# Value ring of four, token-array zeroing on ScalarE's queue, and paired shared feed-forward

## What is computed

```python
# attention on xn = layernorm(x); 16 heads of 16; 16 global keys and a causal window of 32
scores = Q @ K.T * 0.25 + sparse_mask
x = x + softmax(scores) @ V @ Wo.T + xn
# feed-forward on h = layernorm(x)
x = x + h
topk_w, topk_idx = top_k(softmax(h @ gate_w.T), 6)      # 64 experts, weights renormalised
x = x + sum_over_chosen_experts(weight * (silu(h @ w_gate[e].T) * (h @ w_up[e].T)) @ w_down[e].T)
x = x + (silu(h @ sh_gate.T) * (h @ sh_up.T)) @ sh_down.T   # the shared feed-forward, width 352
```

## Time and profile before

| | |
|---|---|
| median of 3 runs | 650.39 us (646.25 to 652.29) |
| the profiled execution, its time | 650.67 us |
| its span, first to last instruction | 649.0 us |
| mean granted TensorE clock | 0.937 of full |
| busy TensorE, VectorE, ScalarE, GpSimd | 561.1, 341.1, 286.8, 338.9 us |
| first phase, to the first expert's transpose | 0 to 308.07 us |
| experts | 308 to 618 us |
| last additions and the output | 618 to 649 us |

### The profile page before, as it was taken

One profiled execution on the slowest core, in us unless ns is written; L12 is line 12 of the kernel. 1 busy time (PEld: TensorE's weight loads), 2 busy tenths in 40 slices (PEclk: granted clock), 3 DMA queues, 4 the chain that ended last, 5 costly groups with the idle time before them and its releaser, 6 DMA issues.

```text
span 649.0 us, 14567 instructions
## 1 busy us (share of the span) xinstructions
PE 561.1 (86%) x4397; PEld 501.1 (77%) x4397; DVE 341.1 (53%) x1024; ACT 286.8 (44%) x847; POOL 338.9 (52%) x337
## 2 busy tenths in 40 slices
PE   2678979999999999662999999999999999999800
PEld 1567969999999998551888888888888888888700
DVE  7245648787888786642444454444444445444300
ACT  2577757777887766101233333333333333333300
POOL 4901145444455454464166666666666666666620
PEclk9978979998999998877899999999999999999955
DMA  8999975262322222123599999999999999999666
GB/s 266 352 396 400 416 260 194 76 208 69 106 76 83 99 83 95 52 87 104 144 232 227 229 239 227 231 237 218 239 227 231 238 222 241 218 240 229 93 163 130
DMA packets 78336, 127.81 MB, mean 197 GB/s; under 512 B 9968, under 2 KB 63024, under 8 KB 74928
## 3 DMA queue, kind: packets, MB, share of 16 engines
q0 software_dynamic: 26768, 59.00, 36.9%
q1 hardware_dynamic: 50432, 67.39, 34.8%
q10 hardware_dynamic: 1088, 0.80, 0.4%
HBM read 61.98 MB, written 66.06 MB: 197 GB/s over the span
## 4 chain that ended last, share of the span: by engine, by line
PE 78%; DMA 8%; DVE 5%; ACT 3%; issue 2%; POOL 2%; SPq 1%; POOLq 0%; ACTq 0%; DVEq 0%
PE PS L636 17%; PE PS L640 9%; PE PS L651 8%; PE PS L653 8%; PE PS L623 4%; PE PS L483 4%; DMA VW<-VS 4%; PE PS L514 4%; PE PS L453 3%; PE PS L573 3%; PE PS L597 3%; PE PS L494 3%; PE PS L583 3%; DMA acc_a<-YE,dest 2%; PE PS L533 2%
## 5 line engine op out<-in xcount | busy, mean ns | idle before, releaser
L1201 POOL DMA_INDIRECT acc_a<-YE,dest x66 | 102.5, 1553 | 81.4 <-issue 67.5
L1188 POOL DMA_INDIRECT expert_rows<-XR,slot x96 | 94.7, 986 | 56.6 <-issue 28.4
L636 PE MATMUL PS<-XET,W 128*128 128x256 f32 x512 | 121.9, 381 | 0.0
L1201 POOL DMA_INDIRECT acc_b<-YE,dest x62 | 96.2, 1551 | 46.8 <-issue 43.2
L636 PEld LDWEIGHTS PS<-XET,W 128*128 128x128 f32 x512 | 97.8, 191 | 13.8 <-issue 0.4
L828 ACT ACTIVATE YE<-PS,wsel 128x256 f32<-128x256 f32 x128 | 53.8, 471 | 114.3 <-PE PS L653 114.3
L1074 DVE TENSOR_TENSOR HE<-SL,PS 128x256 f32<-128x256 f32 x64 | 27.0, 421 | 134.4 <-ACT SL L816 134.4
L651 PE MATMUL PS<-W,HE 128*128 128x256 f32 x256 | 76.3, 380 | 0.0
L653 PE MATMUL PS<-W,HE 128*128 128x256 f32 x256 | 76.1, 379 | 0.0
L713 ACT ACTIVATE SM<-SM,smax 128x112 f32<-128x112 f32 x256 | 75.1, 392 | 1.6 <-DVE smax L941 1.6
L640 PE MATMUL PS<-XET,W 128*112 128x256 f32 x256 | 65.7, 379 | 0.0
(11 more groups left out here) (140 smaller groups left out, 920.0 us busy)
## 6 DMA issues: line engine op xcount, KB each, us to landing
expert_rows<-zero POOLq DMA_DIRECT2D x24, 1088.0 KB, 20.2
W<-in_w SPq DMA_DIRECT2D x64, 368.0 KB, 3.9
XG<-expert_rows SPq DMA_DIRECT2D x64, 272.0 KB, 4.0
W<-in_w SPq DMA_DIRECT2D x64, 128.0 KB, 3.8
W<-in_w SPq DMA_DIRECT2D x64, 48.0 KB, 4.0
acc_a<-zero SPq DMA_DIRECT2D x1, 2432.0 KB, 24.3
X<-in_x SPq DMA_DIRECT2D x4, 512.0 KB, 7.3
acc_b<-X SPq DMA_DIRECT2D x4, 512.0 KB
```

The source lines that it names most:

```text
L636: mm = pe.matmul(PS[:, 2 + q, u * MAIN:u * MAIN + n], W1[:, j, d, u * P:(u + 1) * P], XET[:, q, d, 0:n], start=(d == 0), stop=(d == DC - 1))
L1188: pool.indirect_dma_start(rows, bass.IndirectOffsetOnAxis(ap=slot[:, d2 % UN, k:k + 1], axis=0), XR[:, d2 % UN, :], None, bounds_check=EX ...
L1201: pool.indirect_dma_start(target, bass.IndirectOffsetOnAxis(ap=dest[:, e.slot, t:t + 1], axis=0), YE[:, e.slot, t, :], None, bounds_check= ...
```

## The change

Three edits, in neutral words.

1. VS becomes a ring of four. The copy of block a waits for the transfers of block a-3 instead of a-1.
2. The two transfers that zero acc_a and acc_b's tail leave SP's queue in step 3; ScalarE issues them at the start of its step 7.
3. Blocks 8 to 15 leave the shared feed-forward of the steps (`early` replaces `live`). They are done as four pairs of blocks after the steps' own work, in `drain`: pair p gets gate and up in step 18 + p and down in step 19 + p. A pair's gate and up are six products each over 256 columns into PSUM banks 0 to 3 (free once the last probabilities are copied), its down six products into bank 7. Two halves are signalled apart. X2T holds all 16 blocks. There are 23 steps. The count (line 607) and cmax come after step 21's own work and ahead of that step's `drain`, and the experts still wait for all 16 additions. shared_out of the last two groups of four blocks comes behind the loads of the first expert rows.

```diff
+NL = 8
+NPAIR = (NT - NL) // 2
-        VS = sb("VS", [P, 2, H, HV])
+        VS = sb("VS", [P, UN, H, HV])
-        X2T = sb("X2T", [P, 2, DC, P])
+        X2T = sb("X2T", [P, NT, DC, P])
-            for j in range(NT + LF):
+            for j in range(LP + NT + NPAIR + 1):
                 step(j)
+        def early(b):
+            return 0 <= b < NL
+        def pair_halves():
+            yield 0, slice(0, 2)
+            yield 1, slice(2, FC)
+        def pair_ps(first, h):
+            n = (2 - h) * 2 * P
+            return PS[:, first + h, 0:n].rearrange("p (f t) -> p f t", t=2 * P)
...
@@ SyncE
-                if s == LC:
-                    na = (T + CAP) // P * D // 4
-                    sp.wait_ge(zero_ready, 1)
-                    sp.dma_start(acc_a..., zero...).then_inc(a_ready, 16)
-                    sp.dma_start(acc_b[T:T + CAP, :]..., zero...).then_inc(b_ready, 16)
-                if e2 > 0 and e2 % n == 0:
+                if e2 > 0 and e2 % n == 0 and e2 <= NL:
                     shared_out(e2 // n - 1)
-            shared_out(T // SG - 1)
+            for g in range(NL // (SG // P), T // SG):
+                shared_out(g)
...
@@ TensorE
-                if live(e2):
+                if early(e2):
...
-                if live(e1):
+                if early(e1):
...
+            def pair_first(p):
+                b = NL + 2 * p
+                if p == 0:
+                    pe.wait_ge(pt_evac, RG * NT)
+                else:
+                    pe.wait_ge(sg2_ready, 2 * p)
+                for h, fs in pair_halves():
+                    for f in range(fs.start, fs.stop):
+                        for k in range(DC):
+                            mm = pe.matmul(pair_ps(0, h)[:, f - fs.start, :], shg_s[:, k, f * P:(f + 1) * P],
+                                           X2T[:, b:b + 2, k, :], start=(k == 0), stop=(k == DC - 1))
+                    mm.then_inc(g2_done, 1)
+                if p > 0:
+                    pe.wait_ge(sh2_ready, 2 * p)
...
+            def pair_down(p):
+                pe.wait_ge(sh2_ready, 2 * p + 2)
+                pe.wait_ge(sh_add, NL + 2 * p)
+                for t in range(2):
+                    for f in range(FC):
+                        mm = pe.matmul(PS[:, 7, t * D:(t + 1) * D], SH2[:, f, t * P:(t + 1) * P], shd_s[:, f, :],
+                                       start=(f == 0), stop=(f == FC - 1))
+                mm.then_inc(d2_done, 1)
+            def drain(s):
+                p = s - LP - NT
+                if 1 <= p <= NPAIR:
+                    pair_down(p - 1)
+                if 0 <= p < NPAIR:
+                    pair_first(p)
+            def both(s):
+                step(s)
+                if s == NT + LE:
+                    pe.wait_ge(macc_ready, NT)
+                    pe.wait_ge(pos_read, NT)
+                    pe.matmul(cnt_ps, ones[:, :], Macc[:, :], start=True, stop=True).then_inc(cnt_done, 1)
+                drain(s)
...
@@ ScalarE
+                if s == LF + 1:
+                    act.wait_ge(zero_ready, 1)
+                    act.dma_start(acc_a..., zero...).then_inc(a_ready, 16)
+                    act.dma_start(acc_b[T:T + CAP, :]..., zero...).then_inc(b_ready, 16)
-                    if a >= 2:
-                        act.wait_ge(vw_loaded[(a - 1) % UN], vw_all(a - 1))
+                    if a >= UN:
+                        act.wait_ge(vw_loaded[(a + 1) % UN], vw_all(a + 1 - UN))
...
+                    for h, fs in pair_halves():
+                        act.wait_ge(g2_done, 2 * p + h + 1)
+                        act.activation(TH2[:, fs, :], pair_ps(0, h), ACT.Tanh, scale=0.5).then_inc(th2_ready, 1)
...
@@ VectorE, in its drain, behind the step's own work
+                if 1 <= p <= NPAIR:
+                    dve.wait_ge(d2_done, p)
+                    for t in range(2):
+                        dve.scalar_tensor_tensor(out=X1[:, b, :], in0=PS[:, 7, t * D:(t + 1) * D], ...).then_inc(sh_add, 1)
+                if 0 <= p < NPAIR:
+                    for h, fs in pair_halves():
+                        dve.scalar_tensor_tensor(out=SG2[:, fs, :], in0=TH2[:, fs, :], ...).then_inc(sg2_ready, 1)
+                    for h, fs in pair_halves():
+                        dve.wait_ge(u2_done, 2 * p + h + 1)
+                        dve.scalar_tensor_tensor(out=SH2[:, fs, :], in0=SG2[:, fs, :], ...).then_inc(sh2_ready, 1)
```

More of the change, by code:

```diff
@@ L545, in step @@
                     for k in range(DC):
-                        mm = pe.matmul(gate_ps, X2T[:, d1 % 2, k, :], gate_s[:, k, :], start=(k == 0), stop=(k == DC - 1))
+                        mm = pe.matmul(gate_ps, X2T[:, d1, k, :], gate_s[:, k, :], start=(k == 0), stop=(k == DC - 1))
                 if live(d2):
@@ L600, in step @@
                         mm.then_inc(pv_done, 1)
[L602 to L607, removed]
+            def pair_first(p):
[13 more added lines that the diff above has]
+                for h, fs in pair_halves():
+                    for f in range(fs.start, fs.stop):
+                        for k in range(DC):
+                            mm = pe.matmul(pair_ps(2, h)[:, f - fs.start, :], shu_s[:, k, f * P:(f + 1) * P],
+                                           X2T[:, b:b + 2, k, :], start=(k == 0), stop=(k == DC - 1))
+                    mm.then_inc(u2_done, 1)
+            def pair_down(p):
[19 more added lines that the diff above has]
+                drain(s)
+            steps(both)
             pe.wait_ge(cmax_ready, 1)
@@ L725, in step @@
                 a, b1, b2, c, d1, d2, e1 = (s - k for k in (0, LB, LP, LC, LD, LE, LE))
+                if s == LF + 1:
+                    na = (T + CAP) // P * D // 4
+                    act.wait_ge(zero_ready, 1)
+                    act.dma_start(acc_a.rearrange("(p n) d -> p (n d)", p=P).rearrange("p (n w) -> p n w", w=na),
+                                 zero[:, 0:na].unsqueeze(1).broadcast_to([P, 4, na])).then_inc(a_ready, 16)
+                    act.dma_start(acc_b[T:T + CAP, :].rearrange("(p n) d -> p (n d)", p=P), zero[:, 0:CAP // P * D])\
+                      .then_inc(b_ready, 16)
                 if live(d1):
                     act.wait_ge(x2t_done, d1 + 1)
-                    if d1 >= 2:
-                        act.wait_ge(u_done, d1 - 1)
-                    act.copy(X2T[:, d1 % 2], X2T_ps).then_inc(x2t_evac, 1)
+                    act.copy(X2T[:, d1], X2T_ps).then_inc(x2t_evac, 1)
                 if live(a):
@@ L799, in step, with drain, both @@
                     exps(b1, 3)
-            steps(step)
+            def drain(s):
+                p = s - LP - NT
+                if 0 <= p < NPAIR:
+                    for h, fs in pair_halves():
+                        act.wait_ge(g2_done, 2 * p + h + 1)
+                        if p > 0:
+                            act.wait_ge(sg2_ready, 2 * (p - 1) + h + 1)
+                        act.activation(TH2[:, fs, :], pair_ps(0, h), ACT.Tanh, scale=0.5).then_inc(th2_ready, 1)
+            def both(s):
+                step(s)
+                drain(s)
+            steps(both)
             act.wait_ge(cmax_ready, 1)
```

57 lines of the change are left out of this document (40 added, 17 removed).

## The result

The kernel with the change takes 627.64 us (median of four, 625.78 to 634.56) beside 648.76 for the kernel before (646.25 to 652.29): ratio 0.969, 95% interval 0.960 to 0.978. The forecast was 627 in 616 to 638. The median before is now that of four executions; between the medians the gain is 21.1 us. The profiled execution took 628.47 us with a span of 626.7, 22.3 less than before.

A forecast was written before the change was run, and what follows sets the result against it. Early waits for value windows, then TensorE nearly throughout, were taken to bound the kernel. Gains of 9.6 + 6.2 + 1.0 + 5.1 + 1.6 = 23.5 us off 650.67 gave 627 for the median, 616 to 638 for 8 in 10.

The forecast's parts named there:

- The ring and the moved zeroing: Early part, up to the scores of step 6: waits for value windows go, 9.6 us gained, bounds 3 and 13.
- The stall in step 5: Score matmuls 19.77 us apart in step 5 become 13.4 without the copy's wait: 6.4 us gained, between 5.7 and 7.4.
- The 0.5 us for ScalarE's issues: ScalarE's step 7: two zeroing issues delay work TensorE waits for; 0.5 us charged, between 0 and 3.3.
- Steps 13 to 15: Steps losing shared feed-forward: 43.98 us becomes 37.8, 11.8 for step 13 and 13.0 for the others; 6.2 us gained.
- its sign: What would show it: steps 14 and 15 are 11.8 to 13.6 us with TensorE idle ahead of line 503.
- Step 16 and the drain: Step 16 gains 1.0 us ahead of line 954; from there to the experts 58.4 against 63.49, 5.1 gained, TensorE's pairs last.
- The experts' start: First transpose to second gate product: 5.65 us becomes 4.0 on a warm TensorE, 1.6 us gained (0 to 2).
- Steps 6 to 12: Steps between the early part and step 13: no gain forecast, 0 us.
- The latest window: Rival, chance 0.13: the value product waits for late windows; 3 of the 9.6 us left, about 634.
- the clock did fall: Rival, chance 0.15: the clock stays up in early part, steps 13 to 15 and drain; 32 us gained, 619.
- the pairs' twelve instructions: Rival, chance 0.03: pairs in the drain run at 1.2 GHz throughout, 29.5 us more, 657.
- the pairs alone gained: Rival, chance 0.07: pairs gain nothing, their 31 us cost the drain's gain, steps 13 to 15 stay at 14.1; 641.

The follow-up runs named there:

- extra work: Kernel with the change plus twelve unread gate instructions on TensorE in each of steps 13 to 15: ratio 0.977 on the second chip, 0.974 on the third.
- three pairs: Kernel with the change, but ten blocks keep their shared feed-forward in the steps and six go in pairs: 729.19 us on the second chip, 628.86 on the third.
- the run with the moved wait: Kernel with the change, but TensorE waits for the 16 shared additions only after the first two experts' transposes: 725.31 us, ratio 0.971, on the second chip.

## Why the prediction was right, and where it wasn't

**The ring and the moved zeroing** (9.6 forecast, 10.1 in the profile, 10.7 and 11.4 in time for the runs without pairs). Right, with its reason: the copy's wait was the loss, and a transfer of up to 21.6 us is hidden by two steps. The stall in step 5 was forecast at 6.4, and the step is 6.4 shorter (19.70 to 13.32). The 0.5 us for ScalarE's issues was not needed. That the move could be left out was not said in the prediction; its sum charged both stalls to both edits together. The rule of the Trainium skill (DMA: Bandwidth & Descriptors, "Issuing engines are not separate DMA queues") is that all issuers share the engines; the runs agree: the first stall, 3.72 us, stayed when the zeroing moved, and windows beside acc_a on another queue started late too (3.79 us against 1.13). But acc_a ahead on the windows' own queue held them 13.67 us, and that made the wait of 7.38.

**Steps 13 to 15** (6.2 forecast, 2.7 measured, bounds 3.3 to 8.6). The term failed in size. For steps 14 and 15 the mechanism (an idle time for ScalarE, then a low clock) was the right one; what failed is its size. The prediction took 11.8 us at the full clock, 1.8 more for a fall, and a fall in two of three cases, so 13.0; its sign, 11.8 to 13.6, was missed at 14.12 and 14.03. Both had the fall, it hit the two projections that VectorE, and through the values' copy ScalarE, wait for, and with the clock up they are 12.5, not 11.8 (seen only with the extra work in them). Step 13 was taken at 11.8 with no fall and took 13.14: it had one with no idle time ahead. Where no fall met it, such a step took 11.47 us (the whole change on the third chip) and 11.44 (step 15 of three pairs), so there the 11.8 was sound, though not for ScalarE's sake: TensorE was busy throughout.

```profile
184.46:195.93 11.47, 11.47 (x159) 10.76 (x155) 10.17 (x28) 9.49 (x32) 5.87 (x9) 1.00 0.26 87
```

**Step 16 and the drain** (1.0 and 5.1 forecast, 0.9 and 4.5 measured). Right in its sums: step 18 at 20.4 after step 16 (20.2 forecast, as 11.1 and 9.1; it was 10.20 twice), then 38.6 (38.2), GpSimd's last scatter issued at 47.5 (48.5). That TensorE's pairs end last is shown by taking a pair away: the stretch fell by 6.2 us to GpSimd's floor. One reading was too wide: the clock had fallen before the line 483 of steps 17 to 20, but the last one of the drain took 1.56 us, at 295.98.

**The experts' start** (1.6 forecast, -0.3 measured). Wrong: the prediction had the experts start on a warm TensorE. The handover, two additions on VectorE and a register load of one microsecond, left TensorE idle 1.93 us, and the clock fell again; without that idle time, in the run with the moved wait, the second gate product came 3.3 us earlier. The prediction had priced the handover in the chain but not what an idle time does to what comes behind it, though it had used that very thing two terms earlier.

**Steps 6 to 12** (0 forecast, 3.2 measured). In the kernel before, two of these seven steps were 15.74 us instead of 14.12; in the profile of the kernel after, none was. No edit touches them, and each such step has one fall of the clock (0.89 in the windows). Among the other profiles on the first and third chip one such step is in the run with the ring alone and one in that with the move alone, none with both, two with the pairs alone, one and none in the further runs of the whole change and of extra work, two and none with three pairs. So the two profiles that have both early stalls have two each, the eight others five in all. Whether the change brings any of these 3.2 us, by shifting where the falls come, is open; I count them as luck. Such falls also go with the spread of a kernel's own times: the four executions of the kernel after had mean clocks of 0.939, 0.950, 0.954 and 0.957, and spans of 632.8, 626.7, 625.1 and 624.1 us.

So the forecast's time was right to 0.1% by luck: two misses of 3.5 and 1.9 us met two gains of 3.2 and 1.2 it had not claimed (the last lies in the last additions' landing, 8.65 us against 9.87). Without those two the profile has 17.9 us for the change, the two halves run by themselves 17.8, and the repeat on the third chip 17.0; 23.5 had been forecast.

**The rivals.** None came about. The latest window, 21.6 us, was hidden; the clock did fall in steps 13 to 15 and at the experts' start; the pairs' twelve instructions ran in 2.6 us, at the full clock; and the pairs alone gained 7.1 us.

## What to carry to other kernels

When work is taken out of a step, ask what fills the place: here four microseconds of TensorE work left and two of idle time with a low clock came in, and the step stayed as long. Move work behind the steps only as far as another chain's floor; by the profile four pairs were one too many, and the floor (GpSimd's scatters) could be read from the trace of before. Here a buffer ring that releases the waiting copy was worth more (11.4 us) than taking the transfer in front away (7.3), and with the ring there the move added nothing.

## What the runs showed of the hardware

The clock can fall while TensorE never idles. In the kernel before it fell just ahead of 209.6 us, behind the value products (64 columns of weights, 17 of data) and the score products of lines 597 and 453, with TensorE busy throughout both; step 13 of the kernel after has the same. Windows of the kernel before (us, busy PE, clock, DMA share, GB/s):

```profile
206.20:209.60 3.40, 3.40 (x96) 0.96 0.22 82
209.60:213.00 3.40, 3.40 (x13) 0.54 0.28 105
```

The second chip was 15% slower with the same kernels, 746 us for the one before. Its experts ran at the normal pace (1011 matmul instructions in 200 us, against 1012); its full steps took 22 to 26 us from step 6 on. TensorE waited several times in a step, with nothing in the profile to release it, and the granted clock was low: over steps 6 to 10 of the run with the moved wait, 24.1 us each, TensorE was busy for 20.1, at 0.79. The timeline of the run with the moved wait there (between 100 and 300 us TensorE stood so 37 times ahead of value products alone, 19.6 us in all):

```profile
203.82 0.25 PE L611 MATMUL PS<-VW,PT 112*64 112x17 f32 x2 [0.52 <-issue]
204.58 0.31 PE L611 MATMUL PS<-VW,PT 112*64 112x17 f32 x3 [0.51 <-issue]
205.30 0.35 PE L611 MATMUL PS<-VW,PT 112*64 112x17 f32 x6 [0.41 <-issue]
```

What it waited for is not shown; the part of the program that is written out step by step is hit, and the experts' loop is not. Over the two chips the gains were alike: three pairs 0.975 and 0.969 (16.8 and 19.2 us between medians), extra work 0.977 and 0.974 (16.5 and 16.4).
